# Two fused convolution blocks on one core: the order of the opening loads, the 5x5 weights' split, and two early steps rearranged

## The chip, the cores and the metric

The kernel runs on one core of one Trainium2 chip. The metric is the device time of one execution in microseconds, the median of several runs. In the profile the engines are PE (matrix products), DVE (VectorE), ACT (ScalarE), POOL (GpSimd) and SP (SyncE, which here only issues transfers).

## What is computed

The input x has 16 images of 32 channels, 128 by 128 pixels, in f32. Two blocks follow one another. Each normalizes its input by groups (16 groups, so 2 channels each, over the whole image), convolves it, and adds the result to its input:

```python
x = x + conv3x3(_gn(x), weight * mask)          # mask from sum |weight| and a threshold
x = x + conv5x5(_gn(x), kernel) + bias
def _gn(v, G=16, eps=1e-05):
    g = v.reshape(B_, G, C_ // G, H_, W_)
    return ((g - mean(g)) / sqrt(var(g) + eps)).reshape(v.shape)
```

The second block's group statistics need the whole result of the first for that image.

## The kernel before, in words

The work goes by half images, HALVES = 32 of them; half h is the upper or lower half of image h // 2. The 3x3 convolution of half s and the 5x5 convolution of half s - LAG (LAG = 3) make up step s, so there are STEPS = 35 steps; steps 0 to 2 have only a 3x3 convolution, steps 32 to 34 only a 5x5 one. Every f32 operand is split into two f16 parts, high and low, of which three products are taken: high by high, high by low, low by high.

PE runs its own loop (lines 938 to 989). In a whole step it does the two-row products of the 3x3 convolution (pairs3_high, then pairs3_low, L868), those of the 5x5 one (pairs5_high), then the one-row products of both (singles3, singles5, L886), then pairs5_low. pairs3_high waits for a high image (x3_hi_go) and for free banks (bank3_go); pairs3_low waits for the low image (x3_lo_go); pairs5_high waits for x5_hi_go, which stands for the 5x5 high image and for the evicted banks of the 5x5 convolution before. Before step 3 it has filler products in its waits (keep_warm, L936) and the small products that mix the statistics (L930).

The other engines run programs written out by hand, each strictly in order.

- ACT, step s (lines 495 to 533): evict the 5x5 result of half s - 1 - LAG in four banks into conv_out (take_conv5, L468), give x5_hi_go (L506), gather the statistics that step s - 1 exchanged (L481), take their square roots (L385), normalize a mid image (L438), make the high images (L392, L431), and, where step s exchanges statistics, wait for mv_ready and write them out (spread_stats, L475). The next step's eviction stands behind that wait. Step 1 ends with high_w5 (L423); step 2 is high3(3), the root of image 0's mid statistics, high5_first.
- DVE makes the weights ready (setup3, lines 589 to 608, then the 5x5 maximum and power of two, lines 786 to 789, and s5_lo at L797), takes the statistics of x (stats_in, L615) and of the first block's result (stats_out, L747), evicts the 3x3 result with the addition of x (take_conv3, L739), makes the low images (low3, L719; low5, L727), and computes scales. Group statistics from the third image on go over a small DRAM buffer: bn_aggr on DVE tells ACT by mv_ready, ACT writes mv to DRAM and reads all of it back to every partition, and DVE combines it (group_stats, L660 on).
- POOL clears borders, issues the 16 transfers that move half 1 of the first block's result (L363), then adds conv_out into mid (add_out, L369). LATE = HALVES - LAG = 29: from there on DVE takes half of the banks (take_late, L757; add_late, L764).
- SP issues the loads of x in bands (load_bands, L261) and in own rows (load_own, L250), the moves of the result into bands (L269 to L280) and the stores. At the start it issues the bands of halves 0, 1 and 2, then w5 and bias four times each (L288, L289), then bands 3. ACT issues w3 four times (L486), the threshold (L487) and mix_in (L488).

## Time and profile before

| what | value |
|---|---|
| median of 3 runs | 823.47 us (822.88 to 823.75) |
| the profiled execution | 823.28 us, its span 821.5 us |
| PE busy | 756.0 us, 92% of the span |
| DVE, ACT, POOL busy | 608.8, 333.9, 265.3 us |

The profile shows one execution. Its page gives busy times, the clock granted to PE and the chain of work that ended last; its trace can be asked for each engine's instructions in order of time, for transfers and their landing, and for busy times in chosen stretches. Times in it count from the start of the span.

### The profile page before, as it was taken

To read this page: it belongs to the slowest core of one execution; us is meant where nothing else is said; L and a number is where in the kernel's file an instruction comes from. 1 tells how busy PE (TensorE), PEld (TensorE's weight loads), DVE (VectorE), ACT (ScalarE), POOL (GpSimd) and SP (SyncE) were. 2 spreads that over 40 slices of the span, in tenths; PEclk is the share of its full clock that TensorE was granted. 3 is DMA by queue.
4 is the path that set the end of the run, shared out by engine and by line. 5 is a ranking of instruction groups with operands and counts; after the bars stand their busy time and mean duration, and the time that the engine had idled before them with its cause. 6 is when DMAs were issued, how large, how long until landed. Compare 5 with 4: busy or idle time off the path is not lost.

```text
span 821.5 us, 67804 instructions
## 1 busy us (share of the span) xinstructions
PE 756.0 (92%) x32292; PEld 528.7 (64%) x32292; DVE 608.8 (74%) x970; ACT 333.9 (41%) x289; POOL 265.3 (32%) x161
## 2 busy tenths in 40 slices
PE   0585898899999999999999999999999999998996
PEld 0252484568767667767766766776776676676664
DVE  2888757797878969787879878787878786663341
ACT  0252314344443636344443536353443436362420
POOL 1021034044434332233434343222434343322360
PEclk9997898999999999999999999999999999999998
DMA  9879399989997989899897979898997956673424
GB/s 203 158 143 224 75 217 227 230 205 220 195 222 171 220 195 221 196 218 212 202 217 168 219 183 227 196 225 198 215 219 181 220 116 161 137 167 86 99 51 102
DMA packets 234400, 150.76 MB, mean 184 GB/s; under 512 B 18752, under 2 KB 227712, under 8 KB 230272
## 3 DMA queue, kind: packets, MB, share of 16 engines
q1 hardware_dynamic: 227200, 143.93, 80.8%
q10 hardware_dynamic: 6464, 5.24, 2.7%
q0 software_dynamic: 704, 1.25, 0.6%
q8 instruction: 10, 0.16, 0.1%
q14 instruction: 22, 0.18, 0.1%
HBM read 75.86 MB, written 33.59 MB: 133 GB/s over the span
## 4 chain that ended last, share of the span: by engine, by line
PE 82%; DVE 8%; DMA 4%; issue 2%; DVEq 1%; ACT 1%; ACTq 1%
PE psum L868 63%; PE psum L886 20%; DMA every_mv<-mv_scratch 2%; DVE bn_in L615 2%; DMA thr<-L_conv_threshold_dram 1%; DVE x_lo L719 1%; DVE bn_out L747 1%; DMA mv_scratch<-mv 1%; DVE mid L739 1%; DVEq L742 1%; ACT conv_out L468 0%; ACTq L506 0%; ACTq L486 0%; DVE x_bands L691 0%; ACT x_hi L399 0%
## 5 line engine op out<-in xcount | busy, mean ns | idle before, releaser
L369 POOL TENSOR_TENSOR mid<-mid,conv_out 128x512 f32<-128x512 f32 x120 | 246.0, 2082 | 484.0 <-ACT conv_out L468 484.0
L868 PE MATMUL psum<-x_hi,s_hi 32*64 32x512 f16 x6656 | 201.3, 384 | 18.2 <-ACTq L506 6.2
L868 PE MATMUL psum<-x_lo,s_hi 32*64 32x512 f16 x6656 | 200.1, 383 | 5.9 <-DVE x_lo L719 5.9
L868 PE MATMUL psum<-x_hi,s_lo 32*64 32x512 f16 x6656 | 199.7, 381 | 0.0
L868 PEld LDWEIGHTS psum<-x_hi,s_hi 32*64 32x64 f16 x6656 | 122.0, 105 | 85.9 <-issue 11.2
L868 PEld LDWEIGHTS psum<-x_hi,s_lo 32*64 32x64 f16 x6656 | 133.6, 105 | 53.6 <-issue 4.3
L868 PEld LDWEIGHTS psum<-x_lo,s_hi 32*64 32x64 f16 x6656 | 108.9, 104 | 83.8 <-issue 11.6
L739 DVE SCALAR_TENSOR_TENSOR mid<-psum,unscale,x_own 128x1024 f32<-128x1024 f32 x64 | 79.1, 1278 | 90.5 <-PE psum L886 90.4
L468 ACT ACTIVATE conv_out<-psum,bias,unscale 128x512 f32<-128x512 f32 x120 | 83.7, 777 | 69.7 <-PE psum L868 60.7
L392 ACT ACTIVATE x_hi<-x_bands 128x2304 f16<-128x2304 f32 x31 | 65.6, 2117 | 106.2 <-PE psum L886 106.2
L727 DVE TENSOR_TENSOR x_lo<-mid_bands,x_hi 128x2560 f16<-128x2560 f32 x32 | 93.8, 2932 | 6.9 <-PE psum L868 6.8
L431 ACT ACTIVATE x_hi<-mid_bands 128x2560 f16<-128x2560 f32 x31 | 72.5, 2339 | 50.8 <-PE psum L886 48.8
L385 ACT ACTIVATE root<-gvar 128x1 f32<-128x1 f32 x32 | 6.5, 203 | 207.7 <-DVE gvar L668 175.2
L438 ACT ACTIVATE mid_bands<-mid_bands,nbias,gscale 128x2560 f32<-128x2560 f32 x31 | 78.2, 2524 | 16.0 <-DVE nbias L682 13.6
L747 DVE BATCH_NORM_STATS2 bn_out<-mid 128x6 f32<-128x512 f32 x128 | 79.1, 680 | 4.1
L719 DVE TENSOR_TENSOR x_lo<-x_bands,x_hi 128x2304 f16<-128x2304 f32 x32 | 80.7, 2522 | 0.6 <-ACT x_hi L392 0.2
L615 DVE BATCH_NORM_STATS2 bn_in<-x_bands 128x6 f32<-128x512 f32 x128 | 76.7, 663 | 2.6 <-DMA x_bands<-x_dram 2.6
L886 PE MATMUL psum<-x_hi,s_hi 32*32 32x512 f16 x4096 | 74.3, 378 | 1.8 <-issue 1.7
L886 PE MATMUL psum<-x_hi,s_lo 32*32 32x512 f16 x4096 | 73.4, 376 | 0.0
L691 DVE TENSOR_SCALAR x_bands<-x_bands,gmean,gscale 128x2304 f32<-128x2304 f32 x29 | 67.8, 2339 | 0.5 <-ACT x_hi L403 0.4
L886 PE MATMUL psum<-x_lo,s_hi 32*32 32x512 f16 x4096 | 66.2, 377 | 1.4 <-issue 1.4
L886 PEld LDWEIGHTS psum<-x_hi,s_hi 32*32 32x32 f16 x4096 | 53.6, 88 | 19.7 <-issue 15.7
(91 smaller groups left out, 338.3 us busy)
## 6 DMA issues: line engine op xcount, KB each, us to landing
x_own<-x_dram SPq DMA_DIRECT2D x128, 256.0 KB, 5.0
mid_bands<-mid SPq DMA_DIRECT2D x372, 80.0 KB, 3.4
out_dram<-mid SPq DMA_DIRECT2D x116, 256.0 KB, 5.3
x_bands<-x_dram SPq DMA_DIRECT2D x96, 288.0 KB, 6.1
x_bands<-x_dram SPq DMA_DIRECT2D x32, 272.0 KB, 6.9
mid_bands<-mid SPq DMA_DIRECT2D x124, 64.0 KB, 2.9
every_mv<-mv_scratch ACTq DMA_DIRECT2D x17, 256.0 KB, 4.1
out_dram<-mid SPq DMA_DIRECT2D x20, 128.0 KB, 2.4
```

Of the source, the lines that this page charges most:

```text
L369: nc.gpsimd.tensor_tensor(m, m, conv_out[:, b, :], ALU.add).then_inc(out_added, 1)
L431: nc.scalar.activation(x5_hi[:, :, 2:2 + W], mid_bands[:, k % MB_SLOTS, :, :], ACT.Copy).then_inc(hi5_done, 1)
L438: nc.scalar.activation(v, v, ACT.Identity, bias=nbias[:, at], scale=gscale[:, at]).then_inc(act_scaled, 1)
L468: nc.scalar.activation(conv_out[:, b, :], psum[:, X5_BANK + b, :], ACT.Identity, bias=bias[:, 0:1], scale=unscale[:, 1:2]).then_inc(conv5_ ...
L615: nc.vector.bn_stats(bn_in[:, h // 2 % 2, h % 2, b, :], rows.rearrange("p a w -> p (a w)")).then_inc(bn_x, 1)
L691: nc.vector.tensor_scalar(v, v, gmean[:, 0:1], gscale[:, 0:1], ALU.subtract, ALU.mult).then_inc(scaled, 1)
L719: nc.vector.tensor_tensor(x3_lo[:, :, 2:2 + W], x_bands[:, h % XB_SLOTS, :, :], x3_hi[:, :, 2:2 + W], ALU.subtract).then_inc(x3_lo_go, 1)
L727: nc.vector.tensor_tensor(x5_lo[:, :, 2:2 + W], mid_bands[:, k % MB_SLOTS, :, :], x5_hi[:, :, 2:2 + W], ALU.subtract).then_inc(x5_lo_go, 1)
L739: nc.vector.scalar_tensor_tensor(mid[:, h % MID_SLOTS, at, :], psum[:, X3_BANK + at.start:X3_BANK + at.stop, :], unscale[:, 0:1], x_own[:, ...
L747: nc.vector.bn_stats(bn_out[:, h % 2, b, :], mid[:, h % MID_SLOTS, b, :]).then_inc(bn_mid, 1)
L868: ins = nc.tensor.matmul(psum[2 * C * J:2 * C * (J + 1), bank + i, :].rearrange("p (a w) -> p a w", a=A), w[quad(i), at:at + 2, :].rearran ...
L886: ins = nc.tensor.matmul(psum[quad(j), bank + i, :].rearrange("p (a w) -> p a w", a=A), w[quad(i), at, :], src[quad(i), j + dy:j + dy + A ...
```

## The change

1. Loads. SP issues w3 for two of the four partition groups ahead of everything, ACT the other two, then threshold and mix_in as before; w5 goes ahead of bands 2; the four bias loads move to the ACT queue, behind mix_in, with a semaphore of their own.
2. The 5x5 maximum (largest(w5, 1)) moves from behind low3(2) to between set_apart("x", 0) and the drain that precedes combine(("x", 0)).
3. The split of w5: POOL scales w5 in place (behind its 16 transfers), ACT copies it to f16 (now in step 2, behind high3(3) and ahead of the root of image 0's mid statistics), and POOL subtracts. DVE no longer makes s5_lo.
4. LATE is one less, so half 28 too is evicted and added by halves on DVE and ACT with POOL.
5. In step 4 DVE makes low3(5) ahead of stats_in(6), stats_in(7) and the aggregate; in step 5 (just_now is true there alone) it does take_conv3(5) and low3(6) ahead of stats_in(8), stats_in(9) and stats_out(5).

```diff
-        LATE = HALVES - LAG
+        LATE = HALVES - LAG - 1
@@ sync
+            for q in range(Q // 2):
+                sp.dma_start(w3[quad(q), :, :], w3_dram.rearrange("i a b o -> i (a b) o")).then_inc(w3_loaded, 16)
             load_bands(0)
             load_bands(1)
-            load_bands(2)
             for q in range(Q):
                 sp.dma_start(w5[quad(q), :, :], w5_dram.rearrange("i a b o -> i (a b) o")).then_inc(w_loaded, 16)
-                sp.dma_start(bias[quad(q), :], bias_dram.rearrange("(o a) -> o a", a=1)).then_inc(w_loaded, 16)
+            load_bands(2)
             load_bands(3)
@@ gpsimd, behind the 16 moves of half 1
+            pool.wait_ge(w5_bounded, 1)
+            nc.gpsimd.tensor_scalar(w5[:, :, :], w5[:, :, :], wfac[:, 1:2], None, ALU.mult).then_inc(w5_scaled, 1)
+            pool.wait_ge(w5_hi_made, 1)
+            nc.gpsimd.tensor_tensor(s5_lo[:, :, :], w5[:, :, :], s5_hi[:, :, :], ALU.subtract).then_inc(w5_split, 1)
...
-                if k == LATE:
+                if k == LATE + 1:
+                    pool.wait_ge(bias_loaded, 16 * Q)
                     pool.wait_ge(norm2, HALVES)
@@ scalar, high_w5
-                act.wait_ge(w5_bounded, 1)
-                nc.scalar.activation(s5_hi[:, :, :], w5[:, :, :], ACT.Identity,
-                                     bias=zeros[:, 0:1], scale=wfac[:, 1:2]).then_inc(w5_hi_made, 1)
+                act.wait_ge(w5_scaled, 1)
+                nc.scalar.activation(s5_hi[:, :, :], w5[:, :, :], ACT.Copy).then_inc(w5_hi_made, 1)
@@ scalar
+                if k == 0 and b == 0:
+                    act.wait_ge(bias_loaded, 16 * Q)
...
-            for q in range(Q):
+            for q in range(Q // 2, Q):
                 act.dma_start(w3[quad(q), :, :], w3_dram.rearrange("i a b o -> i (a b) o")).then_inc(w3_loaded, 16)
...
+            for q in range(Q):
+                act.dma_start(bias[quad(q), :], bias_dram.rearrange("(o a) -> o a", a=1)).then_inc(bias_loaded, 16)
...
-                if HALVES < s <= LAST + LAG:
-                    act.wait_ge(late_out, s - HALVES)
+                if LATE + LAG < s <= LAST + LAG:
+                    act.wait_ge(late_out, s - LATE - LAG)
...
                     normalize3(3)
-                    high_w5()
                 elif s == 2:
                     high3(3)
+                    high_w5()
                     take_root(("mid", 0))
@@ vector
             set_apart("x", 0)
+            dve.wait_ge(w_loaded, 16 * Q)
+            largest(w5, 1)
             dve.drain().then_inc(bank3_go, 1)
...
             low3(2)
-            dve.wait_ge(w_loaded, 16 * 2 * Q)
-            largest(w5, 1)
             power_of_two(1)
...
             low3(LAG)
-            dve.wait_ge(w5_hi_made, 1)
-            nc.vector.scalar_tensor_tensor(s5_lo[:, :, :], w5[:, :, :], wfac[:, 1:2], s5_hi[:, :, :],
-                                           ALU.mult, ALU.subtract).then_inc(w5_split, 1)
...
-                if s > HALVES:
+                if s > LATE + LAG:
                     take_late(s - 1 - LAG)
...
-                if s % 2:
+                if s % 2 and not just_now:
                     for h in (s + 3, s + 4):
                         if has3(h):
                             stats_in(h, range(BANKS))
                 if has3(s):
                     take_conv3(s)
+                if just_now:
+                    low3(s + 1)
+                    for h in (s + 3, s + 4):
+                        stats_in(h, range(BANKS))
+                if has3(s):
                     stats_out(s)
                 if s == LAG + 1:
+                    low3(s + 1)
                     for h in (2 * LAG, 2 * LAG + 1):
                         stats_in(h, range(BANKS))
                     aggregate("x", LAG, mv_ready)
...
-                if has3(s + 1):
+                if has3(s + 1) and s != LAG + 1 and not just_now:
                     low3(s + 1)
```

## Rows read from the trace of the kernel before

**Rows 1.** Busy time by stretch: us, PE, PEld, DVE, ACT, POOL, then PEclk, DMA share, GB/s

```profile
136.00:140.00 4.00, 4.00 (x84) 1.72 (x76) 2.61 (x1) 0.00 (x0) 4.00 (x2) 0.50 1.16 207
166.00:756.00 590.00, 589.96 (x26096) 426.04 (x26096) 468.10 (x707) 264.33 (x229) 211.20 (x104) 1.00 0.88 194
760.00:764.00 4.00, 4.00 (x160) 2.36 (x144) 0.69 (x1) 0.00 (x0) 4.00 (x4) 1.00 0.75 190
```

**Rows 2.** DVE in order of time: start us, us, instruction, count, idle before and releaser

```profile
14.94 0.46 DVE L592 TENSOR_REDUCE score<-w 128x9 f32<-128x288 f32 x1 [13.13 <-DMA thr<-L_conv_threshold_dram]
...
22.44 4.84 DVE L615 BATCH_NORM_STATS2 bn_in<-x_bands 128x6 f32<-128x512 f32 x8
...
28.85 0.17 DVE L643 COPY members<-psum 128x16 f32<-128x16 f32 x1 [0.77 <-PE psum L930]
...
57.67 0.98 DVE L569 TENSOR_REDUCE bound<-w 128x1 f32<-128x800 f32 x1
...
68.74 2.56 DVE L719 TENSOR_TENSOR x_lo<-x_bands,x_hi 128x2304 f16<-128x2304 f32 x1
```

**Rows 3.** Opening transfers: issue in time order, then landing: w3's by line, thr's by issue

```profile
3.83 0.46 ACTq L487 DMA_DIRECT2D thr<-L_conv_threshold_dram  x1
...
DMA to landing us min/median/max: 4.8/6.4/7.8
...
thr<-L_conv_threshold_dram ACTq DMA_DIRECT2D x1, 0.5 KB, 11.0
```

**Rows 4.** POOL in order of time: the 16 moves; the one tensor_scalar; one half's additions

```profile
55.71 9.21 POOL L363 DMA_DIRECT2D mid_bands<-mid  x16 [50.73 <-DVE mid L739]
...
757.59 6.88 POOL L369 TENSOR_TENSOR mid<-mid,conv_out 128x512 f32<-128x512 f32 x4 [15.91 <-ACT conv_out L468]
...
782.64 6.41 POOL L377 TENSOR_SCALAR mid<-mid,bias 128x2048 f32<-128x2048 f32 x1
```

**Rows 5.** ACT in order of time: w5's high part, and image 0's mid root

```profile
60.44 1.05 ACT L423 ACTIVATE s_hi<-w,zeros,wfac 128x800 f16<-128x800 f32 x1 [2.53 <-DVEq L789]
...
67.46 0.20 ACT L385 ACTIVATE root<-gvar 128x1 f32<-128x1 f32 x1 [3.95 <-DVE gvar L653]
```

**Rows 6.** PE in order of time, step 3

```profile
71.38 1.85 PE L868 MATMUL psum<-x_lo,s_hi 32*64 32x512 f16 x48
...
81.56 3.20 PE L868 MATMUL psum<-x_hi,s_hi 32*64 32x512 f16 x51 [5.24 <-issue]
```

**Rows 7.** DVE in order of time: one short instruction without, then with POOL at work

```profile
118.90 0.46 DVE L660 SCALAR_TENSOR_TENSOR product<-every_mv,mix_in 128x128 f32<-128x128 f32 x1 [7.53 <-DMA every_mv<-mv_scratch]
...
763.31 1.34 DVE L660 SCALAR_TENSOR_TENSOR product<-every_mv,mix_in 128x128 f32<-128x128 f32 x1 [3.68 <-DMA every_mv<-mv_scratch]
```

**Rows 8.** Steps 4 and 5: DVE, then ACT, then PE, each in order of time

```profile
132.31 2.49 DVE L719 TENSOR_TENSOR x_lo<-x_bands,x_hi 128x2304 f16<-128x2304 f32 x1
...
163.32 2.49 DVE L719 TENSOR_TENSOR x_lo<-x_bands,x_hi 128x2304 f16<-128x2304 f32 x1
...
132.86 2.79 ACT L468 ACTIVATE conv_out<-psum,bias,unscale 128x512 f32<-128x512 f32 x4 [3.02 <-DVE mv L625]
...
163.87 2.79 ACT L468 ACTIVATE conv_out<-psum,bias,unscale 128x512 f32<-128x512 f32 x4 [5.98 <-DVE mv L625]
...
134.86 2.79 PE L868 MATMUL psum<-x_lo,s_hi 32*64 32x512 f16 x48 [3.64 <-DVE x_lo L719]
137.43 5.99 PE L868 MATMUL psum<-x_hi,s_hi 32*64 32x512 f16 x160
...
160.26 2.27 PE L868 MATMUL psum<-x_hi,s_hi 32*64 32x512 f16 x48 [2.46 <-DVEq L742]
162.30 2.47 PE L868 MATMUL psum<-x_hi,s_lo 32*64 32x512 f16 x48
165.87 1.53 PE L868 MATMUL psum<-x_lo,s_hi 32*64 32x512 f16 x48 [1.11 <-DVE x_lo L719]
167.22 4.59 PE L868 MATMUL psum<-x_hi,s_hi 32*64 32x512 f16 x160
```

**Rows 9.** PE in order of time, the starts of steps 32 and 33

```profile
759.61 4.61 PE L868 MATMUL psum<-x_hi,s_hi 32*64 32x512 f16 x160 [2.96 <-ACTq L506]
...
778.25 4.61 PE L868 MATMUL psum<-x_hi,s_hi 32*64 32x512 f16 x160 [1.61 <-ACTq L506]
```

5 lines of the change are left out of this document (4 added, 1 removed).

## Prediction

> **What bounds the kernel now.** I read the busy time by stretch first. From 166 to 756 us PE is busy 589.96 of 590.00 us at a granted clock of 1.00 [rows 1]. The change touches no instruction of PE, so that stretch is worth nothing either way: the kernel's time is the time at which PE gets into it, plus a fixed amount, plus the last steps. So the sum is made of shifts of PE in three places. (a) The opening: the order of time on DVE shows the first real instruction at 14.94 us, after 13.13 us of waiting for the threshold's transfer, and from there DVE, PE and ACT hand the work to each other with waits under a few us. (b) Steps 3 to 5, where PE stops: 5.24 us at "issue" in step 3 [rows 6], 3.64 us for the low image in step 4, 2.46 and 1.11 us in step 5 [rows 8]. (c) The starts of steps 32 to 34, where PE waits 2.96 us and then 1.6 us for ACT's eviction [rows 9]. In (b) the rows to look at are not PE's but ACT's: both times its eviction of the 5x5 banks begins on "DVE mv L625", the aggregate that the exchange waits for, not on PE [rows 8]. ACT is in order, and spread_stats of step s stands ahead of take_conv5 of step s + 1.
>
> **Part 1, the loads.** w3's four transfers landed 4.8 to 7.8 us after issue; the last was issued at about 2.1, so it landed near 9.9. The threshold, issued at 3.83 in the same queue, took 11.0 us: 14.83, 4.9 us behind w3 [rows 3]. After the change two w3 transfers stand ahead of it instead of four, and SP's queue too begins with two small ones instead of bands. ACT's issues take some 0.45 us each [rows 3], so the threshold is issued near 1.65. I let w3 land at about 4.7 (the shortest landing now, 4.8 us, counted from the first issues at 0.7, comes to 5.5 beside bands, less 0.8 without them) and keep the 4.9 us for the threshold: 9.6, a gain of 5.2; I take 5.3. Ends: landing as fast as the quickest w3 now, 1.65 + 4.8 = 6.5, a gain of 8.3; landing still 11.0 us after its issue, 12.65, a gain of 2.2. What is late next: setup3 takes 22.44 - 14.94 = 7.5 us, so statistics begin near 17 us, when the bands of halves 0 and 1 (landed by about 10 and 16 in the trace) are there; SP's two w3 issues cost it 0.9 us, which its queue, never empty before 35 us, hides. w5 ahead of bands 2 makes the same bytes in another order. The bias loads leave SP and are first needed at L468 of step 4, near 100 us: nothing. Part 1: -5.3.
>
> **Part 2, the maximum.** 0.98 us (1.0 with its wait) leaves the path behind low3(2) [rows 2] and goes in front of a wait of 0.77 us, which covers part of it; with the drain behind it some 0.4 us shows. Net -0.6, up to the point where image 0's mid variance is ready. Part 3 swallows this, so it is not a term of its own.
>
> **Part 3, the split of w5 on POOL.** On DVE 1.05 us of s5_lo goes. What comes is a chain POOL, ACT, POOL with two in-order neighbours. In times of the old trace (part 1's shift left out): POOL's 16 moves run 9.21 us from 55.71 [rows 4], now 56.1 to 65.3, and the multiplication stands behind them. The only tensor_scalar of POOL took 6.41 us for 2048 elements a partition, 3.13 ns each: 800 take 2.5 us, to 67.9. ACT's copy of 1.05 us [rows 5] ends near 69.0, and the root of image 0's mid statistics, which ran at 67.46 [rows 5] and could run at 66.8, stands behind it: 69.1. Then POOL subtracts: its additions take 6.88 / 4 = 1.72 us for 512 elements, 3.36 ns each [rows 4], so 2.7 us, 69.05 to 71.75. Beside it DVE wants to run the short steps of scale_of. What such steps do beside POOL is in two rows: the same L660 takes 0.46 us alone and 1.34 us at 763.31, ending when POOL's additions end (757.59 + 6.88 = 764.47) [rows 4, 7]. So I let scale_of's first two-operand step wait until 71.75; with 0.95 us of steps left, low3(3) begins at 72.7 instead of 68.74 [rows 2], 3.95 later. PE's low pass, at 71.38 [rows 6] and not waiting, begins 3.9 later. The high image of the 5x5 (ACT, same scales) is ready at about 75.8, before PE has finished that pass, and s5_lo long before. The 5.24 us at "issue" lies a fixed number of products later, inside the first pass through the 5x5 code, and I let it move along. Part 3 with part 2: +3.9. Ends: +1.5 if POOL's subtraction does not hold DVE (scales at 70.3 instead of 68.8); +6 if the multiplication runs as POOL's additions do at 2.4 us for 512 (step 5's stretch) and the slow clock lasts on.
>
> The Trainium skill, "SBUF — State Buffer", Who interferes with whom, gives a rule for this: VectorE instructions with two SBUF inputs and GpSimd instructions that read SBUF share a port pair under an exclusive lock, held for the whole instruction. Rows 7 agree. By it the sum takes +3.9; without it +1.5, which is a rival below.
>
> **Part 4, step 4.** low3(5), 2.49 us, goes ahead of stats_in(6), (7) and the aggregate [rows 8]. PE's 3.64 us for the low image goes. Late next is x5_hi_go: the aggregate comes 2.5 us later, ACT's eviction with it, to end at 132.86 + 2.79 + 2.5 = 138.15. PE began pairs5_high at 137.43 [rows 8], so it begins 0.8 us later than before, after standing idle from 132.4. PE's clock: at 136 to 140, behind the idle 3.64 us, the granted clock is 0.50, the 1.2 GHz level [rows 1]; the low pass and what followed lost 2.6 us against full speed. A stop of 5.8 us costs about the same again, so +0.8. The exchange of image 3's statistics also leaves 2.5 us later; DVE waits for it with nothing else to do.
>
> **Part 5, step 5.** The chain from that exchange is normalize3(6), take_conv3(5), low3(6), stats_in(8), (9), stats_out(5), aggregates: low3(6) is again 2.49 us ahead of the aggregate that ACT waits for, on top of the inherited 2.5. The eviction ended at 163.87 + 2.79 = 166.66, and PE began pairs5_high at 167.22 [rows 8]. Now 171.65, with the go 171.7: +4.45. PE's waits of 2.46 and 1.11 us and its slow passes at 160.26 and 162.30 go, but they lay before 167.22 and nothing is gained by ending early. Instead PE stands idle some 8 us and restarts at the half clock, where at 167.22 it ran at full speed: +2.1 (between 1.85, lost in step 5 now, and 2.6; less by a little). Parts 4 and 5: +4.45 + 2.1 = +6.5, of which the +0.8 is a part. Ends +4 (no clock loss, a quicker exchange) and +8.5. Behind it PE has slack again, since all it waits for came 5 us later and PE itself 6.5.
>
> **Part 6, LATE.** Step 32's wait of 2.96 us becomes that of step 33, 1.61 [rows 9], since two banks are evicted by each engine. DVE's share ends before the next statistics arrive. The clock is 1.00 there on both sides [rows 1]. -1.35, ends -1.0 and -1.4.
>
> **Sum**, against the profiled execution's own 823.28 us (span 821.5 and 1.8 around it; 0.2 under the median 823.47): -5.3 + 3.9 + 6.5 - 1.35 = +3.75, so 827.0.
>
> **Rivals.** (A) The threshold lands near 6.5 us, gain 8.3: it is the only large unknown of the opening, and small transfers ahead of the bands speak for it; against it stands that it must share with bands for its 4.9 us. 827.0 - 3.0 = 824.0, no change; it decides from a landing before 8.0 us. (B) The two reorderings do what their place suggests: the eviction isn't held by the exchange, PE runs through steps 4 and 5. Then 3.64 + 2.6 and 2.46 + 1.11 + 1.85 us go, -11.7 instead of +6.5: 808.8, faster. Against it: both rows of ACT name DVE's aggregate. A weaker form, where only the clock loss and half of the lateness fall away, gives about 822. (C) POOL's subtraction doesn't hold DVE: 824.6. (D) The threshold still takes 11.0 us: +3.1, 830.1.
>
> **From cases to numbers.** My forecast 0.50 (824.5 to 829.5), A 0.14, B 0.12, C 0.12, D 0.12. A measurement of this kernel can tell about 0.2%, 1.65 us: faster is under 821.8, slower over 825.1. Faster: B, and a fifth of A and C: 0.17. Same: most of A and C, and a twentieth of my forecast: 0.23. Slower: 0.60. The range 820.0 to 831.0 leaves out B's strong form and what lies above D.
>
> **What would show it.** DVE's first instruction behind the threshold near 9.6 us; the root L385 on ACT waiting for high_w5, and low3(3) 3 to 4 us later than part 1 alone would have it; PE's restarts in steps 5 and 6 by "ACTq L506" with 5 to 8 us of idle before them and a granted clock of 0.5 behind; step 32's wait 1.6 us. I am wrong if PE's stops in steps 4 and 5 vanish, if low3(3) isn't late, or if DVE starts before 7 or after 12 us.

## The result, and the profile after

The changed kernel takes 819.94 us, the median of 17 runs (817.41 to 822.91); the kernel before takes 824.01 us in the runs beside it (17 runs, 822.79 to 826.15). The ratio is 0.995 (95% interval 0.9938 to 0.9962): 4.1 us faster. The forecast was 827.0, slower by 3.75, in a range from 820.0 to 831.0. The sign was wrong, and the median lies just under the lower end.

The profiled execution of the changed kernel took 818.68 us, with a span of 816.9 us (before: 823.28 and 821.5). Its page begins so:

```profile
span 816.9 us, 67808 instructions
## 1 busy us (share of the span) xinstructions
PE 755.0 (92%) x32292; PEld 524.7 (64%) x32292; DVE 611.7 (75%) x971; ACT 332.3 (41%) x287; POOL 261.8 (32%) x161
```

The difference of the spans, 4.6 us, can be read off at five points of the two traces (each row is of one execution; how much the first one varies is shown under e8):

| stretch | before | after | difference |
|---|---|---|---|
| start of the span to the first take_conv3 on DVE | 42.56 | 34.54 | -8.02 |
| from there to the low pass of the 5x5 in step 4 on PE | 81.40 | 82.69 | +1.29 |
| from there to PE's one-row products of step 6 | 52.18 | 56.02 | +3.84 |
| from there to the first pass of step 32 | 583.47 | 581.74 | -1.73 |
| from there to the end | 61.9 | 61.9 | 0 |

The forecast's terms in the same order: -5.3 (part 1), +3.9 (parts 2 and 3), +6.5 (parts 4 and 5), -1.35 (part 6). Now the rows. First DVE in order of time, from the score to the low image of half 3 (start us, us, instruction, count, idle time before and its releaser):

```profile
6.02 0.46 DVE L603 TENSOR_REDUCE score<-w 128x9 f32<-128x288 f32 x1 [4.21 <-DMA thr<-L_conv_threshold_dram]
...
16.54 2.47 DVE L626 BATCH_NORM_STATS2 bn_in<-x_bands 128x6 f32<-128x512 f32 x4 [0.54 <-DMA x_bands<-x_dram]
...
34.54 2.48 DVE L750 SCALAR_TENSOR_TENSOR mid<-psum,unscale,x_own 128x1024 f32<-128x1024 f32 x2 [0.73 <-PE psum L901]
...
57.46 0.56 DVE L655 SCALAR_TENSOR_TENSOR product<-members,ones 128x8 f32<-128x8 f32 x1
...
57.95 0.15 DVE L657 SCALAR_TENSOR_TENSOR product<-members,ones 128x8 f32<-128x8 f32 x1
...
60.39 0.16 DVE L686 RECIPROCAL rinv<-root 128x1 f32<-128x1 f32 x1 [1.62 <-ACT root L393]
60.59 1.48 DVE L687 TENSOR_TENSOR newton<-gvar,rinv 128x1 f32<-128x1 f32 x1
...
62.76 2.56 DVE L730 TENSOR_TENSOR x_lo<-x_bands,x_hi 128x2304 f16<-128x2304 f32 x1
```

The first row answers to 14.94 in [rows 2], the last to 68.74. The threshold's group among the transfers of the opening (queue, count, size, us from issue to landing), against 11.0 in [rows 3]:

```profile
thr<-L_conv_threshold_dram ACTq DMA_DIRECT2D x1, 0.5 KB, 4.3
```

The new chain of the weights' split, POOL and then ACT in order of time:

```profile
47.70 9.22 POOL L366 DMA_DIRECT2D mid_bands<-mid  x16 [42.72 <-DVE mid L750]
57.08 2.29 POOL L368 TENSOR_SCALAR w<-w,wfac 128x800 f32<-128x800 f32 x1
60.35 1.70 POOL L370 TENSOR_TENSOR s_lo<-w,s_hi 128x800 f16<-128x800 f32 x1 [0.99 <-ACT s_hi L431]
...
59.40 0.87 ACT L431 ACTIVATE s_hi<-w 128x800 f16<-128x800 f32 x1 [4.19 <-POOL w L368]
60.17 0.19 ACT L393 ACTIVATE root<-gvar 128x1 f32<-128x1 f32 x1
```

The reader is to see one thing here: the newton step, of one element in each partition, lasts 1.48 us, from 60.59 to 62.07, and POOL's subtraction ends at 60.35 + 1.70 = 62.05. Beside POOL's multiplication (57.08 to 59.37) it is otherwise: only the first two-operand step there is longer than elsewhere (0.56 us instead of 0.17), and the next one takes 0.15. PE in order of time, in step 3, at the restarts in steps 4 and 5, at step 6 and at step 32:

```profile
65.37 2.79 PE L883 MATMUL psum<-x_lo,s_hi 32*64 32x512 f16 x48 [3.65 <-DVE x_lo L730]
...
74.59 1.73 PE L883 MATMUL psum<-x_hi,s_hi 32*64 32x512 f16 x51 [1.74 <-issue]
...
79.44 2.61 PE L883 MATMUL psum<-x_hi,s_lo 32*64 32x512 f16 x83 [1.14 <-issue]
...
132.43 6.38 PE L883 MATMUL psum<-x_hi,s_hi 32*64 32x512 f16 x160 [6.61 <-ACTq L517]
...
161.93 6.99 PE L883 MATMUL psum<-x_hi,s_hi 32*64 32x512 f16 x160 [4.72 <-ACTq L517]
...
173.25 0.93 PE L901 MATMUL psum<-x_hi,s_hi 32*32 32x512 f16 x48
...
754.99 4.60 PE L883 MATMUL psum<-x_hi,s_hi 32*64 32x512 f16 x160 [1.61 <-ACTq L517]
```

And ACT in steps 4 and 5: writing image 3's statistics, evicting the 5x5 banks, reading the statistics back, taking the root, and the next eviction:

```profile
129.10 0.35 ACTq L484 DMA_DIRECT2D mv_scratch<-mv  x1
129.56 2.78 ACT L477 ACTIVATE conv_out<-psum,bias,unscale 128x512 f32<-128x512 f32 x4 [5.73 <-DVE mv L636]
133.93 0.35 ACTq L490 DMA_DIRECT2D every_mv<-mv_scratch  x1
142.13 0.20 ACT L393 ACTIVATE root<-gvar 128x1 f32<-128x1 f32 x1 [9.78 <-DVE gvar L679]
...
159.06 2.78 ACT L477 ACTIVATE conv_out<-psum,bias,unscale 128x512 f32<-128x512 f32 x4 [7.91 <-DVE mv L636]
```

The waits for the low image in steps 4 and 5 [rows 8] are gone, and PE stops instead for x5_hi_go (L517), the semaphore behind that eviction. Both evictions still begin on DVE's aggregate (L636).

### The profile page after: what moved, and what is told of

Its sections match the earlier page's. It is cut to its first block, busy times and chain, and to the rows that moved or that the text cites. A ratio compares the mean times of both kernels' runs of the same rounds, so it can differ in the third digit from the quotient of the medians.

```text
span 816.9 us, 67808 instructions
## 1 busy us (share of the span) xinstructions
PE 755.0 (92%) x32292; PEld 524.7 (64%) x32292; DVE 611.7 (75%) x971; ACT 332.3 (41%) x287; POOL 261.8 (32%) x161
## 4 chain that ended last, share of the span: by engine, by line
PE 84%; DVE 5%; DMA 3%; issue 2%; POOL 1%; SPq 1%; ACTq 1%; ACT 1%; DVEq 1%; POOLq 0%
PE psum L883 64%; PE psum L901 20%; DVE x_lo L730 2%; DMA x_bands<-x_dram 1%; DVE bn_in L626 1%; DMA every_mv<-mv_scratch 1%; POOL mid_bands L366 1%; SPq L263 1%; ACTq L517 1%; DVE mid L750 1%; ACT conv_out L477 1%; DVE bn_out L758 0%; DVEq L753 0%; ACT mid_bands L445 0%; ACTq L401 0%
## 5 line engine op out<-in xcount | busy, mean ns | idle before, releaser
L376 POOL TENSOR_TENSOR mid<-mid,conv_out 128x512 f32<-128x512 f32 x118 | 238.4, 2050 | 489.8 <-ACT conv_out L477 489.8
L883 PE MATMUL psum<-x_hi,s_lo 32*64 32x512 f16 x6656 | 197.4, 377 | 1.1 <-issue 1.1
L883 PEld LDWEIGHTS psum<-x_hi,s_hi 32*64 32x64 f16 x6656 | 118.5, 106 | 96.9 <-ACTq L517 18.6
L883 PEld LDWEIGHTS psum<-x_lo,s_hi 32*64 32x64 f16 x6656 | 106.7, 104 | 83.0 <-issue 9.8
L477 ACT ACTIVATE conv_out<-psum,bias,unscale 128x512 f32<-128x512 f32 x118 | 82.3, 776 | 75.1 <-PE psum L883 61.5
```

What stands on the lines that cost most here:

```text
L376: nc.gpsimd.tensor_tensor(m, m, conv_out[:, b, :], ALU.add).then_inc(out_added, 1)
L477: nc.scalar.activation(conv_out[:, b, :], psum[:, X5_BANK + b, :], ACT.Identity, bias=bias[:, 0:1], scale=unscale[:, 1:2]).then_inc(conv5_ ...
L883: ins = nc.tensor.matmul(psum[2 * C * J:2 * C * (J + 1), bank + i, :].rearrange("p (a w) -> p a w", a=A), w[quad(i), at:at + 2, :].rearran ...
```

## The experiments

One table for all of them. The columns are, from each kernel's profiled execution: DVE's first instruction behind the threshold; the first take_conv3 (T0); from T0 to the 5x5 low pass of step 4 (T1); from T1 to the one-row products of step 6; then the median and the ratio to the kernel before, of all runs, with its interval. Kernels e1 to e4, e5 to e8, e9 to e12 and e13 to e15 ran together.

| kernel | first | T0 | T1 - T0 | to step 6 | median us | ratio |
|---|---|---|---|---|---|---|
| before | 14.94 | 42.56 | 81.40 | 52.18 | 824.01 | 1 |
| after | 6.02 | 34.54 | 82.69 | 56.02 | 819.94 | 0.9950 (0.9938 to 0.9962) |
| e1_loads | 8.81 | 36.43 | 80.68 | 52.36 | 817.86 | 0.9919 (0.9903 to 0.9935) |
| e2_oldorder | 9.97 | 37.84 | 81.42 | 53.25 | 816.14 | 0.9902 (0.9884 to 0.9920) |
| e3_oldsplit | 10.94 | 38.83 | 81.15 | 58.63 | 819.01 | 0.9926 (0.9913 to 0.9939) |
| e4_oldlate | 10.28 | 38.15 | 81.08 | 56.06 | 822.91 | 0.9977 (0.9964 to 0.9990) |
| e5_gate | 10.41 | 38.29 | 82.08 | 44.52 | 815.34 | 0.9882 (0.9864 to 0.9900) |
| e6_gate_oldorder | 8.46 | 36.35 | 81.25 | 54.45 | 816.88 | 0.9901 (0.9883 to 0.9919) |
| e7_rootfirst | 10.18 | 38.05 | 81.29 | 57.04 | 818.23 | 0.9918 (0.9904 to 0.9933) |
| e8_thrfirst | 7.49 | 35.36 | 80.87 | 54.83 | 818.39 | 0.9926 (0.9909 to 0.9943) |
| e9_rootlater | 5.96 | 34.60 | 83.73 | 57.84 | 820.10 | 0.9944 (0.9922 to 0.9965) |
| e10_bandsbehind | 5.91 | 34.77 | 82.29 | 51.11 | 814.70 | 0.9880 (0.9851 to 0.9908) |
| e11_w3sp_gate | 5.64 | 35.79 | 81.33 | 46.41 | 814.55 | 0.9874 (0.9847 to 0.9902) |
| e12_s6 | 5.11 | 35.65 | 80.80 | 48.29 | 818.61 | 0.9919 (0.9888 to 0.9949) |
| e13_new_bands | 9.24 | 37.12 | 81.29 | 55.64 | 818.97 | 0.9917 (0.9896 to 0.9937) |
| e14_gate_bands | 10.60 | 38.48 | 82.10 | 41.71 | 815.10 | 0.9874 (0.9848 to 0.9900) |
| e15_w3sp_old_bands | 5.29 | 35.60 | 81.18 | 51.55 | 813.26 | 0.9848 (0.9824 to 0.9872) |

Executions of one kernel differ by 1 to 7.5 us here, so a single profile answers how long a stretch took and what ended a wait, and the medians answer what a part is worth.

### The parts by themselves: e1 to e4

**e1_loads** is the kernel before with part 1 alone.

```diff
+            for q in range(Q // 2):
+                sp.dma_start(w3[quad(q), :, :], w3_dram.rearrange("i a b o -> i (a b) o")).then_inc(w3_loaded, 16)
             load_bands(0)
             load_bands(1)
-            load_bands(2)
...
+            load_bands(2)
@@ scalar
+            for q in range(Q):
+                act.dma_start(bias[quad(q), :], bias_dram.rearrange("(o a) -> o a", a=1)).then_inc(bias_loaded, 16)
```

> The kernel before with part 1 of the change alone (w3 by two queues ahead of the bands, w5 ahead of bands 2, bias on ACT's queue). Theory 1, the sum of the traces: the threshold lands near 6.0 us as in the changed kernel, DVE takes the first 3x3 result near 34.9 us instead of 42.6, and with no split on POOL PE keeps the whole 8 us into the steady stretch: about 8 us under the kernel before. Rival: the loads of the bands and the fetches of PE's code don't come earlier with it, so that half is given back in steps 3 to 5 (longer stop at issue, longer exchanges): about 4 us under.

It came to 0.9919, 6.7 us under the kernel before. DVE began at 8.81 instead of 14.94, T0 came 6.1 earlier, and nothing of that was lost later: T1 - T0 is 0.7 shorter and the stretch to step 6 the same (52.36 and 52.18). The gain lies between the two expectations.

**e2_oldorder** is the changed kernel with DVE's old order in steps 4 and 5.

```diff
-                if s % 2 and not just_now:
+                if s % 2:
...
-                if just_now:
-                    low3(s + 1)
-                    for h in (s + 3, s + 4):
-                        stats_in(h, range(BANKS))
...
                 if s == LAG + 1:
-                    low3(s + 1)
...
-                if has3(s + 1) and s != LAG + 1 and not just_now:
+                if has3(s + 1):
```

> The changed kernel with the old order of steps 4 and 5 on DVE. Theory 1: the new order costs PE 0.9 us at pairs5_high of step 5 (eviction behind the aggregate) and with the clock 2.4 us at step 6, so the old one is 2 to 4 us faster than the changed kernel: 816 to 818. Rival: the quick exchange of step 4 (mv written in 4.8 us instead of 7.7, gathered in 6.2 instead of 8.0) came with the later issue of the new order, behind the bands' transfers, and is lost with the old order: within 1 us of the changed kernel or slower, and the write takes over 7 us again.

0.9902 against 0.9950: the reordering of steps 4 and 5 costs 0.48%, 4.0 us, by the medians. The traces have less for it: the stretch to step 6 is 53.25 us here and 54.83 to 56.06 in the changed kernel, e4 and e8. PE in order of time shows the waits for the low image back, and no stop at the 5x5 pass of step 5, which runs at full speed (granted clock 1.00 from 164 to 168 us):

```profile
130.75 2.79 PE L878 MATMUL psum<-x_lo,s_hi 32*64 32x512 f16 x48 [4.23 <-DVE x_lo L730]
...
156.63 2.15 PE L878 MATMUL psum<-x_hi,s_hi 32*64 32x512 f16 x48 [4.30 <-DVEq L753]
...
163.58 4.59 PE L878 MATMUL psum<-x_hi,s_hi 32*64 32x512 f16 x160
```

ACT, in order of time, shows what else differs. The write, the read and the root of image 3's statistics:

```profile
128.32 0.33 ACTq L484 DMA_DIRECT2D mv_scratch<-mv  x1
...
135.83 0.35 ACTq L490 DMA_DIRECT2D every_mv<-mv_scratch  x1
...
146.53 0.20 ACT L393 ACTIVATE root<-gvar 128x1 f32<-128x1 f32 x1 [14.99 <-DVE gvar L679]
```

From write to root 18.2 us; in the changed kernel 13.0 (129.10 to 142.13).

**e3_oldsplit** is the changed kernel with the split of w5 as it was, on ACT and DVE.

```diff
-            pool.wait_ge(w5_bounded, 1)
-            nc.gpsimd.tensor_scalar(w5[:, :, :], w5[:, :, :], wfac[:, 1:2], None, ALU.mult).then_inc(w5_scaled, 1)
-            pool.wait_ge(w5_hi_made, 1)
-            nc.gpsimd.tensor_tensor(s5_lo[:, :, :], w5[:, :, :], s5_hi[:, :, :], ALU.subtract).then_inc(w5_split, 1)
@@ vector, behind low3(LAG)
+            dve.wait_ge(w5_hi_made, 1)
+            nc.vector.scalar_tensor_tensor(s5_lo[:, :, :], w5[:, :, :], wfac[:, 1:2], s5_hi[:, :, :],
+                                           ALU.mult, ALU.subtract).then_inc(w5_split, 1)
...
```

On ACT, which the lines above leave out, high_w5 scales and converts in one step again and goes back to step 1.

> The changed kernel with w5's split as before (ACT from f32 in step 1, s5_lo on DVE). Theory 1: the root of image 0's mid statistics runs about 2 us earlier, PE's low pass of step 3 starts 2 us earlier, PE gets into steady work 1.4 us earlier: 818.5. Rival: the stop at issue in the first pass through the 5x5 code grows by what the wait for the low image shrinks, since both end with the fetches: within 0.5 us of the changed kernel.

The low image of half 3 came 25.19 us behind T0 instead of 28.22 in the changed kernel, so the split does delay it by 3.0. But T1 - T0 was 81.15, no shorter than in e2, e4 or e8, which have the new split (81.42, 81.08, 80.87). This profile is of its slowest execution (823.93 us): in steps 4 to 6 it lost 6.45 us against before, with an exchange of 16.4 us from write to root where the changed kernel has 13.0. The median lies between the two expectations and decides neither.

**e4_oldlate** is the changed kernel with LATE as before.

```diff
-        LATE = HALVES - LAG - 1
+        LATE = HALVES - LAG
```

> The changed kernel with LATE = HALVES - LAG. Both theories: step 32 starts after a wait of 2.96 us instead of 1.61, 1.35 us slower than the changed kernel, 821.3; nothing else moves.

Step 32 waits 2.93 us instead of 1.61. The ratio is 0.9977 against 0.9950, 2.2 us, with intervals that nearly meet (0.9964 and 0.9962). The trace has 1.3 us for it; nothing in it shows more. The median is 1.6 us above the 821.3 expected.

Together they split the change. By steps from before over e1 and e2 to the changed kernel: part 1 -6.7; parts 2, 3 and 6 together -1.4 (0.9919 to 0.9902); parts 4 and 5 +4.0 (0.9902 to 0.9950). Taking e1 to e4 alone, which ran together, and letting the parts add up: part 1 -0.0081, parts 2, 3 and 6 -0.0017 (e2 less e1), parts 4, 5 and 6 +0.0007 (e3 less e1), parts 2 to 5 +0.0058 (e4 less e1). Solved, parts 2 and 3 come to +0.0017 or +1.4 us, parts 4 and 5 to +3.4, part 6 to -2.8; their sum gives 0.9943 for the changed kernel, which measured 0.9950. Each interval is some 1.3 us to either side, so the second and the last of these are known no better than that. By both ways the forecast's +3.9 for parts 2 and 3 is too much; what speaks for more of it is e7.

### The weights' split and the root: e7, e9

**e7_rootfirst** is the changed kernel with image 0's root ahead of the copy of w5, so that the root doesn't wait for POOL.

```diff
-                    high_w5()
                     take_root(("mid", 0))
+                    high_w5()
```

> The changed kernel with the root of image 0's mid statistics ahead of w5's high part on ACT. Theory of the prediction: the scales come 2 to 2.5 us earlier, PE's low pass of step 3 too, and all of it goes through: 817.5. Rival, from the traces of e1 to e4: PE's first pass through the 5x5 code ends with its stops at issue at nearly the same time whether it began 2 us earlier or not: within 0.8 us of the changed kernel, 819.2 to 820.7.

**e9_rootlater** goes the other way: two more copies of the same size on ACT ahead of the one needed.

```diff
+                for n in range(2):
+                    nc.scalar.activation(conv_out[:, 2 * n:2 * (n + 1), :].rearrange("p b w -> p (b w)")[:, 0:T5 * C],
+                                         w5[:, :, :].rearrange("p t o -> p (t o)"), ACT.Copy)
                 nc.scalar.activation(s5_hi[:, :, :], w5[:, :, :], ACT.Copy).then_inc(w5_hi_made, 1)
```

> The changed kernel with two more copies of w5 on ACT (into an unused tile) ahead of its high part, so that the root of image 0's mid statistics, the scales and DVE's low3(3) come 1.8 us later still. Theory 1, from e3 and e7: from DVE's first 3x3 result to PE's last pass of step 4 it takes 80.7 to 82.7 us whenever low3(3) comes, since the stops at issue in the first pass through the 5x5 code shrink by as much; here 81 to 82.7 again, and 820 us. Rival, the prediction's step: the delay goes through, 82.5 to 84.5 us in this stretch and 821.8 us or more.

In e7 the newton step runs ahead of POOL's subtraction, and PE's low pass begins 28.22 us behind T0 (66.27 less 38.05; 30.83 in the changed kernel). DVE, POOL and then PE in order of time:

```profile
62.80 0.16 DVE L687 TENSOR_TENSOR newton<-gvar,rinv 128x1 f32<-128x1 f32 x1
...
63.91 3.88 POOL L370 TENSOR_TENSOR s_lo<-w,s_hi 128x800 f16<-128x800 f32 x1 [0.99 <-ACT s_hi L431]
...
66.27 1.53 PE L883 MATMUL psum<-x_lo,s_hi 32*64 32x512 f16 x48 [2.66 <-DVE x_lo L730]
...
75.15 3.20 PE L883 MATMUL psum<-x_hi,s_hi 32*64 32x512 f16 x51 [3.99 <-issue]
```

0.16 us here and 1.48 in the changed kernel, for the same instruction: the hold by the subtraction is shown. Here it is turned round: DVE's low3, also of two operands, began at 63.65, just ahead of POOL's subtraction, and the subtraction took 3.88 us instead of 1.70. And PE keeps little of the earlier pass. The stop at "issue" is 3.99 us instead of 1.74. The same in e1, which has the old split (PE, same place):

```profile
75.29 3.19 PE L876 MATMUL psum<-x_hi,s_hi 32*64 32x512 f16 x51 [5.46 <-issue]
```

Put side by side, the start of the low pass and the start of the one-row products behind the 5x5 two-row ones, both counted from T0: before 28.8 and 47.2; e1 28.8 and 47.8; changed kernel 30.8 and 47.4; e2 30.8 and 47.6; e8 30.8 and 47.6. Two microseconds of delay at the first point are nearly nothing at the second. The twelve kernels whose low pass begins 30.8 us behind T0 show how: PE reached the stop between 36.7 and 38.3 us behind T0 and left it between 39.6 and 40.3, whenever it came; in before, e1 and e3 it left at 38.8 to 39.0. The slack has an end: e9, at 32.3 and 48.5, passes on 1.1 of its further 1.5 us, and its T1 - T0 (83.73) is 1.0 longer than the changed kernel's, as the rival had it, though its median (820.10) is what theory 1 had. And e7, at 28.2 and 46.1, gains 1.3 there of which T1 - T0 (81.29) shows nothing against e2, e4 and e8. T1 - T0 has a mean of 81.5 us in those twelve kernels and of 81.1 in before, e1 and e3, so in the traces parts 2 and 3 cost about half a microsecond.

The medians leave more. e7 lies 2.6 us under the changed kernel by its ratio, which is what its first theory, the prediction's step, had foretold (2.4), and e3 lies 2.0 under; no stretch of their profiles shows it (both profiles are of executions 3.6 and 4.9 us above their own medians). But e13 below, which changes neither the split nor the root, lies 2.7 us under too without a stretch that shows it, so a remainder of this size need not come from the edit. Between 0 and some 2.6 us stays open.

### The threshold: e8

**e8_thrfirst** is the changed kernel with the threshold first in ACT's queue.

```diff
+            act.dma_start(thr[:, :], thr_dram.rearrange("(a o) -> a o", a=1).to_broadcast([P, 1])).then_inc(w3_loaded, 16)
             for q in range(Q // 2, Q):
                 act.dma_start(w3[quad(q), :, :], w3_dram.rearrange("i a b o -> i (a b) o")).then_inc(w3_loaded, 16)
-            act.dma_start(thr[:, :], thr_dram.rearrange("(a o) -> a o", a=1).to_broadcast([P, 1])).then_inc(w3_loaded, 16)
```

> The changed kernel with the threshold's transfer as ACT's first instead of its third. Theory 1: the threshold's landing is a matter of what bands stand beside it, which is why the same loads landed it at 6.0, 8.8, 10.0, 10.3 and 10.9 us in five traces; first in the queue it lands with w3, by 6 us, always: DVE's first instruction by 6 us, a median 3 to 4 us under the changed kernel, 816 to 817, and a narrower spread. Rival: the landing varies with the machine and not with the place: 9 to 10 us again and the time within 1 us of the changed kernel.

The threshold then landed 1.8 us after its issue (the transfers of this kernel's opening):

```profile
thr<-L_conv_threshold_dram ACTq DMA_DIRECT2D x1, 0.5 KB, 1.8
```

w3 became the last to land and DVE began at 7.49. By ratios it is 2.0 us under the changed kernel, with intervals that just overlap; that is less than theory 1 expected, and the spread (816.43 to 821.28) isn't clearly narrower.

The table's first column has more to say. Twelve of the kernels have the same loads in the same order as the changed kernel up to the threshold (all but before, e8, e11, e12, e15), and in them DVE began at 5.91, 5.96, 6.02, 8.46, 8.81, 9.24, 9.97, 10.18, 10.28, 10.41, 10.60 and 10.94 us. The middle of these is 9.6, the forecast; the changed kernel's own profile caught one of the earliest, and e8's start, 2.1 us ahead of that middle, fits its 2.0 us. And an early start isn't kept whole: the changed kernel and e10, with T0 under 34.8, have T1 - T0 of 82.7 and 82.3, those later mostly 80.7 to 81.4 (e5 and e14 82.1). The first of the waits that take it back is in the changed kernel's rows, 0.54 us at 16.54 for the bands.

### What holds the eviction in steps 4 and 5: e5, e6

The theory: PE's two stops are there because spread_stats stands ahead of the eviction in ACT's order, so the eviction waits for DVE's aggregate. The rival: the low image or the banks would hold PE just as long.

**e5_gate** is the changed kernel with ACT's write of the statistics behind the next eviction, in these two steps.

```diff
-                if exchanged(s) and s >= LAG:
+                if exchanged(s) and s >= LAG and s not in (LAG + 1, LAG + 2):
                     spread_stats(s)
...
-                if s == LAG:
+                if s in (LAG, LAG + 2, LAG + 3):
                     spread_stats(s - 1)
```

> The changed kernel, but ACT writes the statistics of steps 4 and 5 out behind the next step's eviction instead of ahead of it. Theory 1 (ACT's order makes the new DVE order a loss): both stops of PE by ACTq (6.6 and 4.7 us) go with their slow clock; PE then waits some 3 to 4 us in step 5 for the images that need the exchange: 8 to 11 us under the changed kernel, 809 to 812. Rival: the exchange itself bounds both steps, so PE's stop only moves: 2 to 4 us under, 816 to 818.

PE in order of time, from step 4 to step 7:

```profile
129.12 4.61 PE L883 MATMUL psum<-x_hi,s_hi 32*64 32x512 f16 x160 [0.16 <-ACTq L517]
...
150.89 1.54 PE L883 MATMUL psum<-x_hi,s_hi 32*64 32x512 f16 x48 [2.72 <-DVEq L753]
...
155.95 4.61 PE L883 MATMUL psum<-x_hi,s_hi 32*64 32x512 f16 x160 [0.80 <-ACTq L517]
...
178.77 1.53 PE L883 MATMUL psum<-x_hi,s_hi 32*64 32x512 f16 x48 [3.74 <-ACTq L401]
```

The stops of 6.61 and 4.72 us are 0.16 and 0.80, the passes behind them take 4.61 us instead of 6.38 and 6.99, and the stretch to step 6 shrinks from 56.0 to 44.5. The theory of what holds PE is right, the total it gave (809 to 812) is not. Step 7 then stops 3.74 us for its high image (L401), which on ACT stands behind the roots of the later exchange, and of the 11.5 us gained before step 6 the runs keep 5.6 (0.9882 against 0.9950).

**e6_gate_oldorder** is the same edit with DVE's old order, e2 and e5 together.

> As e5, but with DVE's old order in steps 4 and 5. Theory 1: there PE waits for the low image behind the statistics (4.2 us) and for the 3x3 banks (4.3 us), not for ACT, so the moved write gains nothing: within 1 us of e2's 816.1. Rival, the exchange bounds: the same few us under as e5, so e5 and e6 agree.

0.9901 against 0.9902 for e2: there the edit does nothing, because in the old order DVE's aggregate isn't what comes last. The new order and the move of the write need each other.

### Why the cost was 3.8 and not 6.5: e10, e13

The exchange of image 3's statistics took 13.0 us in the changed kernel and 17.5 to 18.2 in before, e1, e2 and e6 (all of the old order). In the changed kernel the write is issued at 129.10, 4.1 us behind the first of the four band loads of half 9, which SP issues from 124.98 to 130.53; in before, e1 and e2 it is issued 1.4 to 1.9 us behind the first of them (e2: 126.69 and 128.32). If the loads in flight make the difference, then putting them behind the moves of the first block's result must shorten the exchange in the old order too.

**e10_bandsbehind** is e2 with the bands of half 9 behind move_mid(4).

```diff
-                if has3(s + XB_SLOTS - 1):
+                if has3(s + XB_SLOTS - 1) and s != LAG + 1:
                     sp.wait_ge(norm1, s + 1)
...
                     move_mid(s)
+                    if s == LAG + 1:
+                        sp.wait_ge(norm1, s + 1)
+                        load_bands(s + XB_SLOTS - 1)
```

> e2 (the changed kernel with the old order in steps 4 and 5) with the bands of half 9 loaded behind the moves of half 4 instead of ahead of them. Theory 1: the write of image 3's statistics is slow (7.2 to 7.7 us from its issue to the gather's) when it is issued beside a load of bands and quick (4.8) when that is over; here it takes under 5.5 us, image 3's scales come 2 us earlier than in e2, and the kernel is 1 to 2 us under e2. Rival: the write is slow for what stands beside it of any kind, and the moves are as bad: 7 us again and the same time as e2; or the bands are late for stats_in(9) and eat the gain.

ACT, SP and DVE, each in order of time:

```profile
125.69 0.33 ACTq L487 DMA_DIRECT2D mv_scratch<-mv  x1
...
131.59 0.35 ACTq L493 DMA_DIRECT2D every_mv<-mv_scratch  x1
...
137.18 0.20 ACT L396 ACTIVATE root<-gvar 128x1 f32<-128x1 f32 x1 [8.27 <-DVE gvar L682]
...
123.95 13.95 SPq L271 DMA_DIRECT2D mid_bands<-mid  x16
137.95 1.98 SPq L263 DMA_DIRECT2D x_bands<-x_dram  x4
...
145.72 2.47 DVE L629 BATCH_NORM_STATS2 bn_in<-x_bands 128x6 f32<-128x512 f32 x4 [3.29 <-DMA x_bands<-x_dram]
```

Write to root 11.5 us instead of 18.2, with no other edit: band loads ahead of the moves are what makes the exchange this long. The three other kernels with the same edit agree (9.7, 10.4 and 12.2 us in e13, e14 and e15). That the changed kernel's 13.0 comes of the write's later place behind these loads stays argued, and part of the record is against it: e3, e11 and e12 issued the write 3.7, 4.5 and 5.0 us behind the first load and took 16.4, 15.2 and 16.0 us, where e4, e7, e8 and e5, 3.8 to 4.1 us behind it, took 12.6 to 13.8. The stretch to step 6 is 51.1 instead of 53.3, and the price is the last row, 3.29 us of waiting for those very bands. The ratio is 0.9880 against 0.9902, 1.8 us, with overlapping intervals.

**e13_new_bands** makes the same edit on the changed kernel.

> The changed kernel (new order in steps 4 and 5, ACT's write ahead of the eviction) with the bands of half 9 loaded behind the moves of half 4. Theory 1 (those bands make the exchange long): from ACT's write to image 3's root 10.5 to 12.5 us (13.0 in the changed kernel, 17.7 before, 11.5 in e10), so PE's eviction in step 6 comes 0 to 2 us earlier, unless stats_in(9) now waits for its bands: 818 to 820. Rival: the new order alone makes the exchange short; 13 us again.

Write to root 9.7 us, yet the stretch to step 6 is 55.6 instead of 56.0. (The ratio, 0.9917, is 2.7 us under the changed kernel's, more than the trace accounts for.) DVE had the statistics earlier and then waited for PE (DVE in order of time):

```profile
147.48 2.48 DVE L753 SCALAR_TENSOR_TENSOR mid<-psum,unscale,x_own 128x1024 f32<-128x1024 f32 x2 [4.93 <-PE psum L904]
```

In the new order the exchange is no longer what ends last; the held eviction is. That bounds what a shorter exchange can give back there: nothing below 13.0 us, while e3's 16.4 went with a second stop of PE of 8.07 us instead of 4.72.

### Combinations: e11, e12, e14, e15

**e11_w3sp_gate** is e5 with all four w3 transfers on SP and the threshold first on ACT.

```diff
-            for q in range(Q // 2):
+            for q in range(Q):
                 sp.dma_start(w3[quad(q), :, :], w3_dram.rearrange("i a b o -> i (a b) o")).then_inc(w3_loaded, 16)
@@ scalar
-            for q in range(Q // 2, Q):
-                act.dma_start(w3[quad(q), :, :], w3_dram.rearrange("i a b o -> i (a b) o")).then_inc(w3_loaded, 16)
```

> e5 (statistics of steps 4 and 5 written behind the eviction) with all four w3 loads on SP ahead of the bands and the threshold first on ACT. Theory: SP's w3 landed 1.9 us after issue and a threshold issued first 1.8 us, so DVE starts by 5 us in every execution, and the bands of half 1, near 16.5 us, become the bound: first 3x3 result at 34.5 us instead of 38.3, 3 to 4 us under e5, 812. Rival: with SP's bands 0.9 us later nothing is gained beyond e8, 814.5.

DVE begins at 5.64 and the statistics then wait for bands, so that T0 is 35.8: what was late next is now on the path. 0.9874 against 0.9882, which is the same, and not the 3 to 4 us that the theory expected. **e12_s6** is e11 with ACT's high3(7) ahead of the roots in step 6, and DVE's take_conv3(6) and low3(7) ahead of the exchange.

```diff
+                    if s == 2 * LAG:
+                        high3(s + 1)
                     for stat in gathered:
                         take_root(stat)
...
+                if s == 2 * LAG:
+                    take_conv3(s)
+                    low3(s + 1)
                 if gathered:
                     dve.wait_ge(mv_in, 16 * exchange_number(s - 1))
```

> e11 with step 6 rearranged too: ACT makes high3(7) ahead of the roots, DVE takes the 3x3 result of half 6 and makes low3(7) ahead of the exchange. In e5 PE stopped 3.74 us at the start of step 7 for the high image that stands behind the exchange. Theory 1: this stop goes, and PE waits instead at pairs5_high for image 2's mid scales, which come about 5 us of DVE work later than the low image: 0 to 3 us under e11. Rival: DVE's five us ahead of the exchange's sums push both scales back by more than PE gains: 0 to 2 us over e11.

By its median it is 4 us slower than e11 (0.9919 against 0.9874, intervals that just overlap), worse than both expectations: the stop before step 7 is gone and a longer one has come behind it, at the 5x5 pass, with a slow restart (granted clock 0.71 from 185 to 191 us; PE in order of time):

```profile
185.32 6.11 PE L886 MATMUL psum<-x_hi,s_hi 32*64 32x512 f16 x160 [6.51 <-ACTq L515]
```

**e14_gate_bands** joins e5 and e13.

> e5 (new order, write behind the eviction) with the bands of half 9 behind the moves. Theory 1: e5's exchange took 13.8 us and bounded the low image of step 5; at 11.5 PE's stops in step 5 shrink by 2 us, but the exchange of step 5 still bounds step 7: 1 to 2 us under e5, 813.5 to 814.5. Rival: the late bands of half 9 hold stats_in(9), with it the aggregate of step 5, and step 7 starts later by it: no gain on e5 or a loss.

It reaches step 6 soonest of all (41.71), and stops before step 7 for 7.00 us (PE in order of time):

```profile
179.47 2.79 PE L886 MATMUL psum<-x_hi,s_hi 32*64 32x512 f16 x48 [7.00 <-ACTq L404]
```

0.9874, as e5. The rival's cause isn't there (DVE reads the late bands at 150.86 without a wait); the roots of the later exchange, behind which L404 stands on ACT, hold step 7, as theory 1 said. The gain of step 5 is a loss of step 7. **e15_w3sp_old_bands** takes what was left standing: the changed kernel's parts 2, 3 and 6, the loads of e11, the old order in steps 4 and 5, the bands of half 9 behind the moves.

> e10 (old order in steps 4 and 5, bands of half 9 behind the moves) with all w3 loads on SP and the threshold first on ACT, so that the bands and no longer the threshold bound the opening. Theory: the spread of the executions narrows, DVE's first 3x3 result always comes near 35.8 us as in e11 and e12, where e10's profile had a lucky 34.8: median 0 to 2 us under e10's 814.7. Rival: no gain, since an early opening is given back before step 4 (from the first 3x3 result to PE's last pass of step 4 it takes 82.5 us when it is early, 81.2 when it is late).

813.26 us (812.26 to 814.36), 0.9848: 1.5% under the kernel before and the lowest median of all, 1.4 us under e10's as expected, though its interval overlaps those of e5, e10, e11 and e14.

## Why the prediction was wrong, point by point

**What bounds the kernel, and the frame of the sum.** Right. From 174 us to step 32 the difference of the two traces is -1.73 us, of which part 6 is 1.35, and the end is the same to 0.1 us. All else happened ahead of step 6.

**Part 1, -5.3: right in kind, low by 1.4.** e1 measured -6.7. The start of DVE at 9.6 us is the middle of what twelve kernels' executions show, but the steps behind it gain a little too: T1 - T0 is 0.7 shorter in e1. Rival A (a landing near 6.5) is what the profiled execution of the changed kernel happened to show. My text asked whether the threshold lands early or late; it does both, from one execution to the next.

**Parts 2 and 3, +3.9: the mechanism right, the step behind it wrong.** This is the largest of the three misses; alone it takes the sum from +3.75 to about nothing. The chain POOL, ACT, POOL is there as forecast, with smaller terms: multiplication 2.29 (2.5), copy 0.87 (1.05), subtraction 1.70 (2.7, scaled from POOL's additions of 512 elements, which run beside other work). DVE was held until the subtraction ended, and rival C falls: 1.48 us with POOL's subtraction beside the step, 0.16 without (e7). The trace agrees with the lock of the Trainium skill ("SBUF — State Buffer", Who interferes with whom) for the subtraction, to 0.02 us, and not for the multiplication, which reads SBUF too: of DVE's two-operand steps beside it only the first was longer, by 0.4 us. The low image came 2.04 us later behind T0 than before; forecast 3.95. What failed is the sentence "The 5.24 us at 'issue' lies a fixed number of products later, inside the first pass through the 5x5 code, and I let it move along". It didn't move along. It shrank from 5.24 to 1.74 (with a second one of 1.14 behind it) as PE came later, and at the one-row products the 2.0 us of delay were 0.2 (47.2 and 47.4 behind T0). So the end of the stop doesn't follow PE's arrival: the twelve kernels whose low pass begins 30.8 us behind T0 left it within 0.7 us of one another, having reached it within 1.6. The records put it on no engine, and the instruction fetch of PE is the candidate; the Trainium skill ("Runtime: NRT & Kernel Launch", Instruction fetch mechanics) says that a taken branch out of the window forces a fetch by DMA before execution goes on, and PE does enter its loop's 5x5 code here for the first time. No run here separated the fetch from other causes, so this stays argued. What the traces show is that this stop at "issue" is an amount of slack, not a constant, and one that runs out (e9). Right would have been about +0.5 in the sum, with +3.9 as an end. The medians allow 1.4 by e1 to e4 and 2.6 by e7, the traces show about 0.5; how much of the delay the kernel's time really pays stays open between these.

**Parts 4 and 5, +6.5: right in sign and mechanism, too large by 2.5.** PE's waits for the low images went, and it stopped by L517 for 6.61 and 4.72 us (forecast 5.8 and about 8), restarting at the half clock both times, as written (granted clock 0.50 from 132 to 136 us and 0.51 from 160 to 164). By the medians of e2 and the changed kernel they cost +4.0; the two profiles of before and after differ by 3.84, of which e2, with the old order, has 1.1 as well. Rival B falls: e5 shows that it would have needed the write behind the eviction, and that even then part of it comes back in step 7. The term that was mis-sized is the exchange. I let the exchange leave 2.5 us later at its old length, 17.7 us; it took 13.0, so that take_conv3(5) and all behind it were not 2.5 us later. e10 and e13 show that the length hangs on the band loads; that it was short here because it left later is argued, and e3, e11 and e12 don't fit it. e3, where it took 16.4, lost 6.45 in that stretch: my figure, where the exchange is nearly as long as I had it.

**Part 6, -1.35.** The row came as forecast (1.61). The runs give 2.2 (e4) or 2.8 (e1 to e4), known to some 1.3 us or more either way; the trace shows nothing beyond 1.35.

**The range and the chances.** By the steps over e1 and e2 the misses are 1.4 (part 1), 3.95 (parts 2, 3 and 6: +2.55 forecast, -1.4 measured) and 2.5 (parts 4 and 5), all of one sign, 7.85 together: the whole way from +3.75 to -4.1. Part 1 lay within its ends and parts 4 and 5 at the lower one; part 3 fell below its end of +1.5, which took in only the hold on DVE and not that PE might not pay for a late image. Each of these figures rests on medians of 5 to 17 executions and is known to some 1.3 to 2 us. And the range didn't use the ends it had: -8.3 + 1.5 + 4 - 1.4 comes to 819.1, but I stopped at 820.0, as if three terms would not fall short together. With 0 for part 3 the ends reach 817.6, and "faster" deserves far more than 0.17.

## What to carry to other kernels

Before a delay is added to the sum, look at the next stop on the same engine: if it is one that the profile calls "issue", or any wait whose end is set elsewhere, take the delay out of it first, and keep both cases in the range. An order that puts work ahead of a statistic or an exchange moves the cost to whatever stands behind that wait on the in-order engine that sends it; here the eviction behind ACT's write, so the two must be moved together, and the step after next must be looked at before the gain is counted. A round trip through DRAM had no length of its own here (9.7 to 18.2 us, write to root): ask what transfers will be in flight when it starts. And where executions differ by 5 us for a transfer that lands early or late, a median of six decides little under 2 us.

## What the runs showed of the hardware

- The same loads in the same order let a 512-byte transfer land 4.1 to 9.2 us after its issue (twelve kernels; e10 and e3 are the ends), 11.0 with four w3 transfers ahead of it, and 1.8 when it was first in its queue (e8, e11, e12, e15). In one execution or another that is 5 us of the kernel's time.
- A write of 2 KB and its read back, up to the root, took 17.5 to 18.2 us issued 1.4 to 1.9 us behind the first of four band loads (before, e1, e2, e6), 12.6 to 16.4 issued 2.9 to 5.0 us behind it (the nine others with the loads in their old place), and 9.7 to 12.2 with them moved behind (e10, e13, e14, e15).
- POOL's subtraction beside a VectorE instruction of two operands and one element: 1.48 us instead of 0.16, so the small size of the VectorE instruction gave no protection. Where VectorE's two-operand instruction came first (e7), the subtraction took 3.88 us instead of 1.70. POOL's multiplication by a per-partition factor held only VectorE's first step beside it, for 0.4 us.
- The stop of PE at "issue" in its first pass through the 5x5 code was 1.64 to 5.59 us (e12 and e3). It was 4.0 to 5.6 us where the 109 products ahead of it began about 30 us behind T0 (before, e1, e3, e7) and 1.6 to 3.3 where they began 33 to 35 us behind T0 (the thirteen others).
- The stops of PE of 6.6 and 4.7 us in steps 4 and 5 of the changed kernel cost 1.8 and 2.4 us more in the 160 products behind each (6.38 and 6.99 us instead of 4.6, at a granted clock of 0.50 and 0.51 around the restarts); in the other kernels with these stops 1.3 to 2.9 more. Behind a stop of 0.8 us (e5) they took 4.61.
